# One block of attention and experts: score tiles issued in two groups, the residual sum ahead of the last probability copies, k and q projected apart

## The reference, cut to what matters

```python
h = layernorm(x) * (1 + ca) + sa
q, k, v = split(h @ W_qkv)              # 16 heads x 64
q, k = rotary(q), rotary(k)
scores = where(causal, q @ k.T / 8, -1e9)
out = softmax(scores) @ v               # per head
x = x + ga * (out @ W_out)
h = layernorm(x) * (1 + cb) + sb
y = sum over the top 2 of 8 experts of gate_e * (gelu(h @ w_up[e].T) @ w_down[e].T)
return x + gb * (layernorm(y) + h)
```

## Time and profile before

| | us |
|---|---|
| median of 3 runs (993.32 to 998.24) | 996.21 |
| profiled execution | 990.0 |
| its span | 988.2 |
| PE busy | 903.2 (91%), 6278 matmuls |
| DVE busy | 770.1 (78%) |
| ACT busy | 743.5 (75%) |
| POOL busy | 570.8 (58%) |

### The profile page before, as it was taken

How to read it: one execution, slowest core, us unless ns; L and a number is a source line. 1 busy time by engine, 2 the same in 40 slices (tenths; PEclk the granted TensorE clock), 3 DMA queues, 4 the chain that set the end, 5 groups by cost and what they waited for, 6 DMA issues and landing times. The chain is left out here.

```text
span 988.2 us, 21752 instructions
## 1 busy us (share of the span) xinstructions
PE 903.2 (91%) x6278; PEld 657.7 (67%) x6278; DVE 770.1 (78%) x2328; ACT 743.5 (75%) x2070; POOL 570.8 (58%) x687
## 2 busy tenths in 40 slices
PE   4699999999999999999999999999999878999920
PEld 3467667676776677777767677677676556888820
DVE  7577777777877787877778778777887679899847
ACT  4488878878787887788778878787878755777725
POOL 1445456645666467657765764657566356765532
PEclk9999999999999999999999999999999989999975
DMA  8234443334344434433343344343333357999844
GB/s 258 84 94 105 111 110 98 95 94 105 95 111 117 116 97 119 118 97 95 109 114 96 102 122 119 101 114 112 106 94 96 98 199 269 311 317 331 296 143 128
DMA packets 124580, 135.78 MB, mean 137 GB/s; under 512 B 13837, under 2 KB 108443, under 8 KB 120496
## 3 DMA queue, kind: packets, MB, share of 16 engines
q1 hardware_dynamic: 118768, 122.61, 42.8%
q0 software_dynamic: 4544, 8.93, 2.7%
q10 hardware_dynamic: 1152, 2.85, 0.8%
HBM read 51.72 MB, written 39.49 MB: 92 GB/s over the span
## 5 line engine op out<-in xcount | busy, mean ns | idle before, releaser
L1357 POOL TENSOR_TENSOR four<-four 128x512 f32<-128x512 f32 x128 | 161.2, 1280 | 276.1 <-DMA four<-four 138.8
L1276 DVE CUSTOM_DVE_ANT_0 ps<-ps,tri 128x512 f32<-128x512 f32 (+3 forms) x512 | 239.0, 520 | 73.2 <-PE ps L1070 73.1
L1172 ACT ACTIVATE prob<-ps,nmax 128x512 f32<-128x512 f32 (+3 forms) x512 | 264.7, 534 | 4.1 <-DVE nmax L1276 3.3
L1091 PE MATMUL ps<-ident,prob 128*128 128x128 f32 x1280 | 191.1, 279 | 6.5 <-ACT prob L1172 2.4
L1091 PEld LDWEIGHTS ps<-ident,prob 128*128 128x128 f32 x1280 | 142.8, 141 | 55.5 <-ACT prob L1172 26.4
L1361 POOL TENSOR_TENSOR qk_lo<-four,qk_hi 128x512 fp32r<-128x512 f32 x128 | 163.1, 1296 | 0.1
L1193 ACT COPY probt<-ps 128x512 f32<-128x512 f32 (+2 forms) x256 | 125.2, 522 | 41.1 <-PE ps L1091 41.1
L1113 PE MATMUL ps<-probt,val 128*64 128x512 f32 (+3 forms) x1024 | 152.0, 439 | 0.2 <-ACT probt L1193 0.2
L1200 ACT CAST qk_hi<-four 128x512 fp32r<-128x512 f32 x128 | 79.4, 620 | 94.3 <-POOL four L1357 92.8
L1263 DVE TENSOR_TENSOR four<-ps,turn_s 128x1024 f32<-128x1024 f32 x64 | 78.4, 1225 | 54.8 <-PE ps L1035 50.3
L1113 PEld LDWEIGHTS ps<-probt,val 128*64 128x64 f32 x1024 | 67.8, 136 | 73.7 <-issue 59.5
(11 more groups left out here) (276 smaller groups left out, 2234.9 us busy)
## 6 DMA issues: line engine op xcount, KB each, us to landing
four<-four SPq DMA_DIRECT2D x252, 128.0 KB
wt<-parts SPq DMA_DIRECT2D x24, 1024.0 KB, 6.7
slots<-fill SPq DMA_DIRECT2D x64, 288.0 KB, 2.8
parts<-split SPq DMA_DIRECT2D x64, 128.0 KB, 2.3
wq_lo<-parts SPq DMA_DIRECT2D x6, 1024.0 KB, 6.3
hb<-h_hi SPq DMA_DIRECT2D x64, 64.0 KB, 2.3
hb<-h_lo SPq DMA_DIRECT2D x64, 64.0 KB, 2.0
plain<-results SPq DMA_DIRECT2D x8, 512.0 KB, 7.5
```

What stands on the lines that cost most here:

```text
L1091: mm = e.transpose(ps[:, PT + at % 2, at_block * P:(at_block + 1) * P], prob[:, unit, kk * P:(kk + 1) * P], ident[:])
L1172: e.activation(prob[:, unit, 0:w], ps[:, bank_s(idx) + j, 0:w], ACT.Exp, bias=nmax[:, q.par, idx, j:j + 1], scale=-1.0, accum_out=den[:, q ...
L1276: e.tensor_tensor_reduce(block_, block_, tri[:, S - w:S], -1.0, HIGHEST, ALU.add, ALU.min, nmax[:, q.par, idx, j:j + 1]).then_inc(v_max, 1)
L1357: e.tensor_tensor(qk[:, cols], tt[:, cols], ur[:, cols], op=ALU.add).then_inc(g_qk, 1)
```

## The change

On PE the slot is written anew. The projection is cut into `pe_k` and `pe_q`, with turn "0" between them. Score tiles 0 and 1 stand back to back ahead of the value product, tiles 2 and 3 behind it, and all four are in the slot (before, the fourth stood at its end). The turned sums go to bank 6 instead of W1. On ACT all eight exponentials of a pair are in one slot; the copies "0", "2a", "2b", "1" are ACT's and "3a", "3b" are DVE's; the v copy stands between the two rounded halves. On DVE the residual sum comes ahead of the copies "3a" and "3b", and these are last in the slot. In spare slots PE now waits for DVE's copy of "3a".

```diff
-            def pe_qk(e, q):
+            def pe_k(e, q):
                 ...
                 if due(n - 2):
                     e.wait_ge(v_acc, n - 2)
                 ...
+
+            def pe_q(e, q):
+                n = q.n
                 e.wait_ge(a_v, min(n + 2, NV))
                 ...
@@ def pe_turn_prob(e, q, u):
                 if u == "3a":
-                    if due(2 * n):
-                        e.wait_ge(v_ev, 2 * n)
+                    if due(4 * n - 1):
+                        e.wait_ge(a_ev, 4 * n - 1)
+                    if due(n):
+                        e.wait_ge(a_r, n)
                 elif u == "3b":
                     if due(4 * n):
                         e.wait_ge(a_ev, 4 * n)
-                elif u == "2a":
-                    e.wait_ge(v_ev, 2 * n + 1)
+                elif u in ("0", "2a"):
+                    e.wait_ge(v_ev, 2 * n + {"0": 1, "2a": 2}[u])
                 else:
-                    e.wait_ge(a_ev, 4 * n + {"0": 1, "2b": 2, "1": 3}[u])
+                    e.wait_ge(a_ev, 4 * n + {"2b": 1, "1": 2}[u])
@@ def pe_turn_sum(e, q):
                 e.wait_ge(a_rep, q.n + 1)
-                e.wait_ge(v_tk, min(q.n + 3, STEPS))
+                e.wait_ge(a_ev, 4 * q.n + 3)
                 for i in range(TB):
-                    mm = e.transpose(ps[:, W1, i * P:(i + 1) * P],
+                    mm = e.transpose(ps[:, PT, i * P:(i + 1) * P],
@@ def pe_values(e, q):
                 e.wait_ge(v_t, min(n + 3, STEPS))
+                e.wait_ge(v_tk, min(n + 3, STEPS))
@@ def pe_slot(e, i, c):
                 if q0.live:
-                    pe_qk(e, q0)
+                    pe_k(e, q0)
                 if q2.live:
                     spare_read(e, i, c - 1)
                     pe_turn_prob(e, q2, "0")
+                if q0.live:
+                    pe_q(e, q0)
+                if q2.live:
                     pe_turn_prob(e, q2, "2a")
-                if q1.live:
-                    pe_scores(e, q1, 0)
-                if q2.live:
                     pe_turn_prob(e, q2, "2b")
                     pe_turn_prob(e, q2, "1")
                     pe_turn_sum(e, q2)
                 if q1.live:
+                    pe_scores(e, q1, 0)
                     pe_scores(e, q1, 1)
                 if q2.live:
                     pe_values(e, q2)
                 if q1.live:
+                    pe_scores(e, q1, 2)
+                    pe_scores(e, q1, 3)
                     pe_turn_prob(e, q1, "3a")
-                    pe_scores(e, q1, 2)
+                    pe_turn_prob(e, q1, "3b")
                 if q2.live:
                     pe_out(e, q2)
-                if q1.live:
-                    pe_turn_prob(e, q1, "3b")
                 if v.live:
                     pe_v(e, v)
                 if c in SPARE:
                     if q1.live:
-                        e.wait_ge(a_ev, 4 * q1.n + 1)
+                        e.wait_ge(v_ev, 2 * q1.n + 1)
                     elif q2.live:
-                        e.wait_ge(v_ev, 2 * q2.n + 2)
+                        e.wait_ge(a_r, q2.n + 1)
                     route_pe(e, i, c)
-                if q1.live:
-                    pe_scores(e, q1, 3)
@@ def act_slot(e, i, c):
                 if q2.live:
-                    act_exp(e, q2, 5)
-                    act_exp(e, q2, 6)
-                    act_exp(e, q2, 7)
                     act_store(e, q2, "0")
+                    act_rep(e, q2)
                     act_store(e, q2, "2a")
-                    act_rep(e, q2)
+                    act_store(e, q2, "2b")
                     act_store(e, q2, "1")
                     act_r(e, q2)
                 ...
                     act_exp(e, q1, 3)
-                    act_store(e, q1, "3a")
                 route_act_part(e, i, c, 1)
                 ...
+                if q1.live:
+                    for unit in range(4, NU):
+                        act_exp(e, q1, unit)
                 if q0.live:
                     act_hi(e, q0, 1)
-                    act_hi(e, q0, 0)
                 if v.live and (i, c) != (0, 2):
                     act_v(e, v)
+                if q0.live:
+                    act_hi(e, q0, 0)
                 ...
-                if q1.live:
-                    act_exp(e, q1, 4)
@@ def dve_slot(e, i, c):
                 if q2.live:
-                    dve_peak(e, q2, 6)
-                    dve_peak(e, q2, 7)
+                    dve_rden(e, q2)
                 if q0.live:
                     dve_u(e, q0)
-                if q2.live:
-                    dve_rden(e, q2)
-                if q0.live:
                     dve_t(e, q0, 1)
                     dve_t(e, q0, 0)
                 ...
-                if q2.live:
-                    dve_store(e, q2, "2b")
                 if q1.live:
-                    ...
+                    for unit in range(4):
+                        dve_peak(e, q1, unit)
                 route_dve(e, i, c)
                 ...
                 if q2.live:
                     dve_ot(e, q2)
                 if q1.live:
-                    dve_peak(e, q1, 4)
-                    dve_peak(e, q1, 5)
+                    for unit in range(4, NU):
+                        dve_peak(e, q1, unit)
                 if q2.live:
                     dve_acc(e, q2)
                 if q1.live:
+                    dve_store(e, q1, "3a")
                     dve_store(e, q1, "3b")
```

More of the change, by code:

```diff
@@ L1189, in act_store @@
                 e.wait_ge(p_t, 6 * n + TURNS.index(u) + 1)
-                if u == "3a" and due(n - 1):
-                    e.wait_ge(p_vp, n - 1)
                 dst, src = turned(q, u)
@@ L1209, in act_r @@
                     e.wait_ge(v_ot, q.n)
-                e.copy(rs[:], ps[:, W1, :]).then_inc(a_r, 1)
+                e.copy(rs[:], ps[:, PT, :]).then_inc(a_r, 1)
             def act_rep(e, q):
@@ L1287, in dve_store @@
                 e.wait_ge(p_t, 6 * n + TURNS.index(u) + 1)
-                if u == "3b" and due(n - 1):
+                if u == "3a" and due(n - 1):
                     e.wait_ge(p_vp, n - 1)
```

## The result

The changed kernel takes 1015.97 us (median of 4 runs, 1010.55 to 1016.72) against 995.88 (4 runs, 993.32 to 998.24): a ratio of 1.0191, 95% interval 1.0147 to 1.0234. The profiled execution took 1016.47, its span is 1014.7; before it was 990.0 and 988.2. The profiled execution before is 5.9 faster than the median before, the one after 0.5 slower than its median, so the two profiles differ by 26.5 where the medians differ by 20.1.

What follows compares the result with a forecast made beforehand. PE's own stream was taken to bound the kernel, with new waits consuming the saved steps. From the profiled 990.0, +25 for slots and -12 for vanished waits gave 1003; adding 6.2 gave 1009 for the median, range 970 to 1028.

Steps and rivals of the forecast that it cites:

- The saved steps: On PE, array-shape steps per slot fall from nine to four; its stream becomes 10.37 us, 0.87 less than 11.24.
- First wait: In each slot PE's turn "1" waits 0.45 us for ACT's copy of "2a" to free bank 7.
- Second wait: At the slot's end PE's next k waits 0.25 us for DVE's sum into x, which reads its bank.
- The walk: A start-by-start reckoning of a quiet slot from k to k: 11.21 us against 11.24 before.
- Third wait: In spare slots PE waits 0.85 us before the routing step for DVE's copy of "3a".
- The routing results behind turn "0": After spare slots turn "0" waits for bank 6: +0.34 us behind c = 4 and 7, +0.15 behind c = 2.
- Slots in sum: Attention slots cost 3.13 us more per round of 8, bounds 1.5 to 4.5; 25 us over 8 rounds.
- What goes: PE's waits for the v copy (8.6 us) and POOL's low part (3.7) disappear: -12 us.
- The last step: From profiled execution to median: 6.2 us, the median's excess before, takes 1003 to 1009.
- the first: Rival: faster, the new PE waits covered by earlier DVE work or cheaper restarts; 966 the likelier end; chance 0.24.
- The second: Rival: no change, spare slots cost half, so 25 us becomes 12, giving 996; chance 0.17.
- The third: Rival: slower by more, ACT falls behind; 0.3 us in each slot adds 19, giving 1028; chance 0.12.

Runs made afterwards that it cites:

- run 4: The changed kernel with the turned sums between score tiles 0 and 1: 1039.58 us, ratio 1.0459 to the kernel before.
- run 3: The changed kernel with ACT's copy of turn "2a" cut from 384 to 128 columns for all pairs but the first two: 1005.28 us, ratio 1.0100.
- run 2: The changed kernel with the out product (W_out) first, ahead of turns "3a" and "3b" on PE: 1000.53 us, ratio 1.0063.
- Run 1: The changed kernel with DVE's copy of "3a" first, ahead of the residual sum: 997.46 us, ratio 1.0011.
- run 6: The changed kernel with DVE's copy of "3a" ahead of the sum and ACT's reader of bank 6 ahead of the second rounded half: ratio 0.9918.
- run 7: The changed kernel with W_out product earlier, "3a" copy ahead of sum in spare slots, bank 6 reader earlier, POOL's W_out weights ahead of c = 6 counts: ratio 0.9912.
- run 5: The changed kernel with q projected right behind k again, ahead of turn "0": ratio 1.0439 to the kernel before.

## Why the prediction was right

Forecast 1009 (970 to 1028), slower with 0.59; measured 1016.

- **The saved steps.** Four instead of nine. Right in kind, and run 4 prices a step at 0.17, between the 0.15 and 0.20 read from the earlier trace rows. PE's stream without its two waits is 11.18 - 0.50 - 0.26 = 10.42 in the quiet slot shown, against 10.37.
- **First wait, "1" behind ACT's copy of "2a".** 2.84 against 2.83; run 3 shows that it is on the path.
- **Second wait, k behind the sum.** 11.18 against 11.21; run 2 takes it away, and the slot ends at 10.97. The walk gave 10.96 twice, as the end of v on PE and as ACT's loop; the rows of run 2 show that it is PE's stream that ends the slot there.
- **Third wait, spare slots.** 12.22, 12.20 and 12.18 in c = 2, 4, 7 against 12.20. Run 1 takes it away: these slots 11.3 or 11.4.
- **The routing results behind turn "0".** c = 5 11.56 against 11.21 + 0.34 = 11.55. But the sum takes the slot before as 11.24, and c = 5 was 11.43 and c = 3 11.50: they rose by 0.13 and fell by 0.02, where the sum has +0.30 and +0.11. What I didn't see is that this wait and the third share their time: the reader on ACT sits at a fixed place, so PE's earlier step only waits longer for it. Runs 1 and 6 show that.
- **Slots in sum.** +3.13 a round expected, +2.99 by the medians in the table. That these are so close is in part luck: the 0.30 too much in c = 3 and 5 is made up for the most part by c = 0 (+0.79 for +0.69) and c = 6 (+0.64 for +0.51).
- **What goes.** Mis-sized: I credited 12 us for late DMAs no longer felt. The mean slot rose by 0.28, 2.24 a round, where the medians rose by 2.99. If the difference is the late slots that are gone, which is an inference, the credit is 0.75 a round, 6 us.
- **Outside the slots.** Not in the sum at all: 5.2 between the last k and the experts, 4.6 in the experts. With the second kernel's drain at full clock (out first, 34.0) about 2 us of the 5.2 are the longer chain of the last pairs, which now have all eight exponentials behind one another; the rest stands beside the lower clock. That the change causes the lower clock isn't shown, and the 4.6 doesn't come of it in every run: out first and sum between hold the change too and have the experts at 194.5, with 0.83 in their first 20 us like the kernel before, while copy first has 198.9 with 0.74.
- **The last step, luck.** Against the profiled execution the forecast was 1003 and 1016.5 was measured: 13.5 off, 3.7 in the slots (16.7 against 13) and 9.8 outside them. I then added 6.2, because the median before lay that much above the profile before. The median after lies 0.5 below its profile, so this addition made up 6.7 of the 13.5, and 1009 looks closer to 1016 than the working was.

Of the rivals, the first (the three waits covered by something I place wrongly) is refuted by runs 1 to 3. The second (spare slots at half the cost) is refuted by +0.47 to +0.64 in c = 2, 4, 6 and 7. The third (ACT behind in every slot) is refuted by a quiet slot of 11.17; ACT comes late only once the waits are taken away. The rule that a change of tiling mode drains TensorE (the Trainium skill, TensorEngine Tiling (Array Packing), Key Properties) agrees with the trace and with run 4, and would alone have given the wrong sign.

## What to carry to other kernels

A reordering that saves time on the busiest engine is worth only what the chains through the other engines leave of it: write one slot down start by start, with the wait, the release and the copy's own length at each bank that is used again, before believing the saved sum. A copy that frees a shared bank belongs ahead of work whose result is wanted later; here one exchange on DVE and one on ACT turned +1.9% into -0.8%. When a wait is taken away, look for the reader with a fixed place in its engine's order; here it took over in three of eight slots.

## What the runs showed of the hardware

- Two score tiles back to back cost no step between them: tile 1 starts 0.82 after tile 0 (495.70 - 494.88), where a 512-key tile with the step out of it took 0.90.
- The walk's two numbers at "1" were each a little off and cancelled. The copy of "2a" is the first of the two in this row of the kernel after:

```profile
493.27 0.86 ACT L1196 COPY probt<-ps 128x384 f32<-128x384 f32 x2
```

With the mean of 0.48 for such a copy it ends at 493.75, not after 0.52, and "1" starts at 493.89, 0.14 behind it, not 0.05.
- DVE and POOL: in four c = 1 slots of run 7 and four of run 5 DVE is late with a maximum and goes on within 0.02 us of the end of POOL's W_out weights.
- The kernel before took 995.39 us on one chip and 1024.35 on another. The profiles taken on the second have their excess in the experts (220.1 us in the last run against 194.4 to 199.0 on the first); the kernel before was not profiled there.
